# Moving VectorE's accumulation of the transposed states to the end of each half step

## The reference

```python
# Mamba block, on the layer-normed x: D_MODEL 256, d_inner 512, N = 16 states
h = rms_norm(x) * norm_w;  u, z = split(h @ in_proj.T)
uc = silu(conv4(u));  dt, B, C = split(uc @ x_proj.T);  dt = softplus(dt @ dt_proj.T + b)
# per state n: h_n[t] = exp(dt*A_n)[t] * h_n[t-1] + (dt*B_n*uc)[t];  y[t] = sum_n C_n[t] * h_n[t]
out = ((y + uc*D) * silu(z)) @ out_proj.T + residual
x1 = x + layer_norm(out)
# feed forward, on the layer-normed x1: 256 -> 1024 -> 1024 -> 1024 -> 256, ternary weights
h = silu(w1 x) * (w2 x);  h = gelu(h1 h);  h = gelu(h2 h);  x2 = x1 + layer_norm(w3 h)
```

## Time and profile before

| | |
|---|---|
| Median of 3 runs | 2146.95 us |
| Time of the profiled execution | 2145.72 us |
| Its span in the trace | 2143.9 us |
| Mean granted TensorE clock | 0.826 |
| TensorE / VectorE / ScalarE / GpSimd busy | 71% / 78% / 58% / 43% |
| Round that scans chunk 10 | 1294.5 to 1416.4 us |

### The profile page before, as it was taken

One profiled execution on the slowest core, in us unless ns is written; L12 is line 12 of the kernel. 1 busy time (PEld: TensorE's weight loads), 2 busy tenths in 40 slices (PEclk: granted clock), 3 DMA queues, 4 the chain that ended last, 5 costly groups with the idle time before them and its releaser, 6 DMA issues.

```text
span 2143.9 us, 30164 instructions
## 1 busy us (share of the span) xinstructions
PE 1518.3 (71%) x9080; PEld 1332.4 (62%) x9080; DVE 1678.4 (78%) x2943; ACT 1238.1 (58%) x2654; POOL 925.8 (43%) x392
## 2 busy tenths in 40 slices
PE   4655676777767677776667777676777767777765
PEld 2212566767666666676666776576666666666765
DVE  3779978888788878988788887888789887887620
ACT  4443655756466575657457564756656574665544
POOL 1324353534436354444436344453544445363411
PEclk8876778878789888887789787888878988888888
DMA  3321100101000010100001010100101010010000
GB/s 114 98 79 40 30 22 17 37 17 35 19 31 22 16 37 17 36 17 31 22 16 36 17 36 18 31 22 16 37 17 36 17 34 19 16 32 20 17 7 7
DMA packets 38920, 63.65 MB, mean 30 GB/s; under 512 B 5216, under 2 KB 19424, under 8 KB 38640
## 3 DMA queue, kind: packets, MB, share of 16 engines
q10 hardware_dynamic: 18944, 33.83, 5.2%
q1 hardware_dynamic: 19696, 26.02, 3.8%
HBM read 55.38 MB, written 4.46 MB: 28 GB/s over the span
## 4 chain that ended last, share of the span: by engine, by line
DVE 29%; PE 23%; issue 21%; ACT 16%; POOL 7%; DMA 1%; DVEq 1%; ACTq 1%; POOLq 0%; SPq 0%
DVE S L1018 12%; PE fP L501 6%; PE fP L502 6%; DVE acc L1032 4%; PE sT L525 4%; POOL Glo L449 3%; ACT dA L752 3%; PE hP L489 3%; PE fP L489 2%; DVE Rw L1143 2%; POOL S L430 2%; POOL X L438 2%; DVE x L1130 2%; DVE X L1082 2%; DVE uc L1077 2%
## 5 line engine op out<-in xcount | busy, mean ns | idle before, releaser
L430 POOL TENSOR_TENSOR S<-X,Bs 128x1024 f32<-128x1024 f32 x256 | 614.7, 2402 | 903.0 <-PE sT L525 749.2
L752 ACT ACTIVATE dA<-delta,A 128x256 f32<-128x256 f32 x1024 | 446.0, 469 | 720.6 <-DVE S L1018 682.3
L1018 DVE TENSOR_TENSOR_SCAN S<-dA,carry,S 128x256 f32<-128x256 f32 x1024 | 708.1, 732 | 135.1 <-ACT dA L752 100.6
L501 PE MATMUL fP<-Ghi,w_h 128*128 128x256 f32 x2048 | 600.0, 322 | 88.2 <-DVE uc L1104 56.5
L502 PE MATMUL fP<-Glo,w_h 128*128 128x256 f32 x2048 | 572.2, 309 | 0.0
L501 PEld LDWEIGHTS fP<-Ghi,w_h 128*128 128x128 f32 x2048 | 447.8, 219 | 105.7 <-DVE uc L1104 51.9
L525 PE MATMUL sT<-ident,S 128*128 128x128 f32 x2048 | 353.9, 305 | 216.3 <-DVE acc L1032 190.0
L502 PEld LDWEIGHTS fP<-Glo,w_h 128*128 128x128 f32 x2048 | 447.5, 219 | 0.0
L525 PEld LDWEIGHTS sT<-ident,S 128*128 128x128 f32 x2048 | 263.4, 156 | 293.9 <-DVE acc L1032 194.7
L1032 DVE SCALAR_TENSOR_TENSOR acc<-sT,CT,acc 128x512 f32<-128x512 f32 x480 | 348.3, 728 | 66.5 <-PE sT L525 65.5
L449 POOL TENSOR_TENSOR Glo<-Rw,Ghi 128x1024 fp32r<-128x1024 f32 x96 | 236.5, 2465 | 239.7 <-ACT Ghi L916 126.8
(11 more groups left out here) (127 smaller groups left out, 1947.2 us busy)
## 6 DMA issues: line engine op xcount, KB each, us to landing
Bs<-b_rows ACTq DMA_DIRECT2D x128, 256.0 KB, 3.2
Rw<-in_h SPq DMA_DIRECT2D x11, 512.0 KB, 3.3
xh<-in_x SPq DMA_DIRECT2D x16, 256.0 KB, 4.1
xt<-in_x SPq DMA_DIRECT2D x16, 256.0 KB, 4.1
out<-x SPq DMA_DIRECT2D x16, 256.0 KB, 3.4
x<-in_h SPq DMA_DIRECT2D x5, 512.0 KB, 3.3
Rw<-in_w SPq DMA_DIRECT2D x4, 512.0 KB, 5.6
w_in<-in_in_proj SPq DMA_DIRECT2D x1, 1024.0 KB, 5.9
```

The costliest lines, as they stand in the source:

```text
L430: pool.tensor_tensor(S[slot(par, n)][:, :, :], X[par][:, :, :], row[:, None, :].broadcast_to([P, DT, T]), ALU.mult).then_inc(scan_pool.sem, 1)
L501: pe.matmul(dst, w[:, i, cols_], hi[:, i, :], start=(j == 0), stop=False)
L752: a = act.activation(dA[half][:, i, :], delta[par][:, d, :], ACT.Exp, scale=A[:, d * N + n:d * N + n + 1])
L1018: a = dve.tensor_tensor_scan(s[:, d, :], dA[half][:, i, :], s[:, d, :], carry[:, n, d:d + 1], ALU.mult, ALU.add)
```

## The change

The gathers of the scan move from behind the two scans to the end of the half step, behind `split_input`, `end_step`, `tail_step` and `head_step`. The gathers of the last states of the previous chunk, in half steps 0 and 1, stay where they were. No wait, tile or instruction is added or removed on any engine.

```diff
                     if scan:
                         back(c, par, n, hs % 2)
-                    if hs % 2 == 0:
-                        if scan and n >= 2:
-                            gather(c, par, n - 2, 1)
-                        if tail and n == 0:
-                            gather(c - 1, 1 - par, N - 2, 1)
-                    else:
-                        if scan and n >= 1:
-                            gather(c, par, n - 1, 0)
-                        if tail and n == 0:
-                            gather(c - 1, 1 - par, N - 1, 0)
-                            gather(c - 1, 1 - par, N - 1, 1)
+                    if tail and hs == 0:
+                        gather(c - 1, 1 - par, N - 2, 1)
+                    if tail and hs == 1:
+                        gather(c - 1, 1 - par, N - 1, 0)
+                        gather(c - 1, 1 - par, N - 1, 1)
                     if tail and hs == 15:
                         split_input(c - 1, 1 - par)
...
                     if head:
                         head_step(c + 1, 1 - par, hs, prepare if head_seq_start is None else head_seq_start)
+                    if scan and hs % 2 == 0 and n >= 2:
+                        gather(c, par, n - 2, 1)
+                    if scan and hs % 2 == 1 and n >= 1:
+                        gather(c, par, n - 1, 0)
```

## The result

The changed kernel takes 2209.5 us (median of 4 runs, 2201.48 to 2213.25) against 2145.07 us before (4 runs beside it); the ratio is 1.0294, 95% interval 1.0258 to 1.0330. The forecast was 2200 us, 54.6 us more than before; measured are some 64. The profiled execution took 2212.72 us, its span is 2210.9 us.

What follows compares the result with a forecast made beforehand. VectorE leads (78% busy, TensorE 71%), nothing at peak; their loop runs against TensorE, whose transposes wait for gathers. 0.7 + 0.65 - 1.05 + 3.6 = 3.9 us over 14 rounds, +54.6 on 2145.7: 2200 us, range 2140 to 2226.

Steps and rivals of the forecast that it cites:

- The bound and the sign: VectorE and TensorE loop runs against TensorE; late gathers delay transposes and `h1` behind them: slower, 0.77.
- Half steps 3 to 11, +0.7: Late `out`, L1053 freed, L1119 held, L986 waiting longer, L1130 freed: +0.7 us a round, bounds -0.5 and +1.5.
- the first link, `out`: Half step 3's later gather starts `turn` of half step 4 1.1 us later, and so `out` behind it.
- Half steps 14 and 15, +0.65: Gathers come on top of taps still waiting for ScalarE's L817: +0.65 us a round, bounds +0.3 and +0.7.
- Half steps 16 to 21, -1.05: L1159 freed of GpSimd, less a Silu wait (-1.4), later branches +0.35: -1.05 us a round, bounds -1.8 and -0.3.
- Half steps 24 to 30, +3.6: Late gathers of 25 and 28 delay transposes, `h1` blocks and L1089: end of `h1` +3.6 us a round.
- the four cases: `h1` blocks behind the transposes of 26 and 29, each 2.37 or 3.94 us by clock: 2.1, 3.6, 3.7 or 5.2.
- The sum: The four stretches together: +3.9 us a round over 14 rounds, +54.6 us, to 2200 us; forecast's chance 0.62.
- The rule on the clock: Pauses between matmul bursts lower TensorE's clock; both `h1` blocks slow, 5.5 us a round, 2223 us; rival's chance 0.15.
- The two pauses: New TensorE pauses from the change: about 3.0 us before half step 26 and 2.4 us before 29.

Runs made afterwards that it cites:

- experiment 1: Kernel before, with the gather last in half steps 25 and 28 alone: 2206.1 us, ratio 1.0283.
- experiment 4: Changed kernel, with TensorE's transposes behind the block of `h1` in half steps 26 and 29: 2167.4 us, ratio 1.0103 to the kernel before.
- experiment 6: Changed kernel plus matmuls nobody reads, 12 in half step 25 and 9 in 28: 2174.8 us, ratio 1.0128 to the kernel before.
- Experiment 10: Kernel before, with the gather last in half steps 3 and 6 alone: 2134.4 us, ratio 0.9949.
- experiment 7: Kernel before, with the gather last in half steps 12 to 22 alone: 2152.8 us, ratio 1.0033.
- experiment 5: Changed kernel plus 20 matmuls nobody reads in half step 25: 2221.9 us, ratio 1.0345 to the kernel before.
- experiment 9: Kernel before, with the gather last in half step 6 alone: 2112.8 us, ratio 0.9848.

## Why the prediction was right, point by point

*The bound and the sign.* Shown. TensorE's waits for gathers rose from 190 to 332 us; experiments 1, 4 and 6 put the loss behind the transposes of 26 and 29. The prediction lets it reach the next round by the end of `h1`. It reaches VectorE by L1089 as well, whose waits grew by 32.5 us in all; the last L904, which follows VectorE's scans in ScalarE's order, waits only 0.45 us for `h1`, where it waited 0.33. The two ways end together, and no run takes them apart.

*Half steps 3 to 11, +0.7.* From the scans of 2 to those of 11 the round of chunk 10 lost 1.0 us, within its bounds; the median of chunks 1 to 14 is 1.4, twice the forecast, and chunks 1, 5, 6, 13 and 14 lost 1.8 to 2.3, beyond its upper bound of 1.5. Its lower bound does not follow from its terms, which give -0.3 + 0.65 - 1.5 = -1.15 with nothing lost in 9, not -0.5. Each piece is in the rows: `out` late (L1114 waits 1.99), L1053 free, L1119 held, L986's wait up from 1.02 to 1.66, L1130 free and an L1005 held. Experiment 10 shows the first link, `out`. What I did not see is that without half step 3 there is a gain in half step 6 to be had.

*Half steps 14 and 15, +0.65.* Only 0.1 in this round, under its lower bound of +0.3. The taps waited for L817 as told (2.86 us), but TensorE's clock was high there and the GpSimd products with it came earlier, so the four taps took 5.10 and not 5.39 us. In experiment 7, with the clock as before, half step 14 cost the 0.66.

*Half steps 16 to 21, -1.05.* Measured -0.45 up to the scans of 22. L1159 and Silu came as predicted. The missing term is ScalarE: the decays of 21 came 0.70 us late.

*Half steps 24 to 30, +3.6.* From the scans of 25 to the last L904, +2.75. Of the four cases it was the one with a slow block in 26 (1443.32 to 1447.22, 3.90 us) and a fast one in 29 (2.40). Smaller than forecast by 0.85: 0.54 of it because GpSimd held L1082 for less (2.06 in place of 2.60 us), which paid for most of the gather's 0.65, and the rest behind the transposes of 30, which no longer wait.

*The sum.* 3.9 us a round was forecast. In a typical round it is 3.3 to 3.5; where the kernel before had quicker rounds (chunks 5, 6, 13 and 14) it is 4.6 to 5.5, and the mean over chunks 3 to 14 is 3.97. That a typical round comes so near is in part luck: in chunk 10 the terms are off by +0.3, -0.55, +0.6 and -0.85. I counted 14 rounds, which lost 57.6 us (chunk 1 alone 6.1); what I left out lost 9.4 more, 3.3 up to the end of the first round, which has no tail, and 6.1 in the last with what follows. The span grew by 67 us (the medians by 64); of the 12 between that and the forecast, 9.4 are these and 3.0 the size of the terms.

*The rule on the clock.* The two pauses were predicted at 3.0 and 2.4 us and are 3.38 and 2.59. The prediction reads the Trainium skill (TensorE: Matmul & The Clock Gate, "HAM oscillation — how this bites in real kernels") so that both blocks run slow. For the second block that goes beyond the page, whose case is a wait for DMA longer than this pause. By the runs the pauses do lower the clock (experiments 5 and 6: filled pause, 1.00), but the same pause of 2.59 us was followed by a high clock in the changed kernel and by a low one in experiments 1 and 5. The prediction's rows had this already, had more of them been read: it says that only a wait of nearly 3 us was followed by the lower level in its round, but there is one of 2.73 us too, and in other rounds of the kernel before

```profile
1296.55 1.12 PE L525 MATMUL sT<-ident,S 128*128 128x128 f32 x4 [2.73 <-DVE acc L1032]
...
1277.21 1.11 PE L525 MATMUL sT<-ident,S 128*128 128x128 f32 x4 [1.89 <-DVE acc L1032]
...
827.74 0.66 PE L525 MATMUL sT<-ident,S 128*128 128x128 f32 x4 [2.85 <-DVE acc L1032]
```

a wait of 1.89 us was followed by the lower level and one of 2.85 us by the full clock. The wait of 1.88 to 1.92 us in half step 27 stands in 12 rounds of that trace; 5 went on at the lower level and 7 at the full clock. So the length of a pause alone does not decide here; what else does, these runs don't tell.

*Open.* Parts do not add up (60 + 14.6 against 64; 8 + 0 against 14.6). The mean clock moves with most edits, and I have not separated its share in half steps that were not edited. As a mean it does not rank the kernels: it is 0.839 in experiment 5, which is slower than the changed kernel at 0.827.

## What to carry to other kernels

A wait on one engine is not a hole to be filled for free: before moving an instruction behind other work, look at what the other engine has queued behind the thing that waits for it, here a block of 16 matmuls and the next transposes behind four transposes. Where the consumer has a longer wait one step later anyhow, as behind half step 6, the late gather costs nothing there. Move such an instruction one place at a time: of fifteen places two made the loss, one made a gain of 1.5%, and all at once hid the gain. Where the consumer's queue is the path, changing its order is a cure for the same lateness, for two thirds of it here (experiment 4).

## What the runs showed that I had not expected

Work on TensorE that nobody reads made a kernel 35 us faster (2209.5 to 2174.8), with the granted clock at 1.00 in the two blocks behind it and at 0.847 against 0.827 as a mean; some 21 of the 35 us lie in half step 28, behind the first of these blocks, and 9 in half step 6. And an edit in one half step moved the mean clock of the whole run from 0.826 to 0.853 (experiment 9), and nearly half of its gain lies in half steps that it does not touch.
